# Two of the three one-column operations of attention's output norm go from GpSimd to VectorE

## The reference, cut to what matters

```
x = x + layernorm(attention(layernorm(x)))
x = x + layernorm(ffn(layernorm(x)))

def layernorm(x, eps=1e-05):
    m, v = mean(x), var(x)            # over the 128 columns
    return (x - m) / sqrt(v + eps)
```

```
local   = softmax(masked(q @ k.T * scale)) @ v
remote  = softmax(masked(rq @ rk.T)) @ rv @ rout_w + rout_b
gate    = sigmoid(local @ gl_w + remote @ gr_w)
result  = (gate * local + (1 - gate) * remote) @ out_w + out_b
```

## Time and profile before

| | |
|---|---|
| time, median of 3 runs | 557.9 us (557.33 to 559.46) |
| the profiled execution | 559.23 us |
| its span, first to last instruction | 557.4 us |
| mean granted TensorE clock | 0.956 |
| steady part of attention (s = 3 to 29) | about 110 to 341 us of the span |

### The profile page before, as it was taken

How to read it: one execution, slowest core, us unless ns; L and a number is a source line. 1 busy time by engine, 2 the same in 40 slices (tenths; PEclk the granted TensorE clock), 3 DMA queues, 4 the chain that set the end, 5 groups by cost and what they waited for, 6 DMA issues and landing times. The chain is left out here.

```text
span 557.4 us, 16662 instructions
## 1 busy us (share of the span) xinstructions
PE 506.9 (91%) x5277; PEld 312.7 (56%) x5280; DVE 424.0 (76%) x1954; ACT 298.3 (54%) x820; POOL 338.8 (61%) x799
## 2 busy tenths in 40 slices
PE   8878679999999999999999998869999999999991
PEld 3434324556556665555555665535677677577671
DVE  5986696988888888998899887645647777675655
ACT  2665305888888888888888888713212211211110
POOL 4799202688888888688888889960122343333241
PEclk9999855999999999999999999989999999999997
DMA  4466450332112332123331100000000000000001
GB/s 128 137 214 176 150 98 2 101 92 69 49 27 59 81 63 64 38 41 63 62 64 40 27 4 4 4 1 1 0 1 1 20 19 0 19 20 0 20 19 38
DMA packets 49058, 28.09 MB, mean 50 GB/s; under 512 B 6808, under 2 KB 48056, under 8 KB 48976
## 3 DMA queue, kind: packets, MB, share of 16 engines
q1 hardware_dynamic: 47648, 26.73, 19.0%
q10 hardware_dynamic: 1328, 0.36, 0.3%
HBM read 17.90 MB, written 8.91 MB: 48 GB/s over the span
## 5 line engine op out<-in xcount | busy, mean ns | idle before, releaser
L1096 DVE CUSTOM_DVE_ANT_0 added<-psS,maskq 128x256 bf16<-128x256 f32 x512 | 200.5, 414 | 34.8 <-PE psS L937 21.9
L1316 ACT ACTIVATE probs<-psST 128x512 f32<-128x512 f32 x240 | 143.2, 597 | 43.2 <-PE psST L973 41.7
L973 PE MATMUL psST<-qst,kst 50*128 50x128 bf16 x992 | 101.0, 222 | 0.0
L937 PE MATMUL psS<-kst,qst 48*128 48x256 bf16 x448 | 91.5, 286 | 2.4 <-DVE rowmax L1096 1.3
L994 PE MATMUL psPV<-probs,vst 128*10 128x128 f32 x1984 | 79.9, 277 | 11.9 <-POOL probs L1231 8.1
L1760 ACT ACTIVATE hT<-fpsH 128x512 f32<-128x512 f32 x32 | 19.1, 597 | 121.7 <-PE fpsH L1504 121.7
L1228 POOL TENSOR_SCALAR_AFFINE_SELECT probs<-probs 128x256 f32<-128x256 f32 x150 | 61.7, 412 | 4.3 <-ACT probs L1316 4.1
L1231 POOL TENSOR_SCALAR_AFFINE_SELECT probs<-probs 128x256 f32<-128x256 f32 x150 | 61.2, 408 | 0.0
L937 PEld LDWEIGHTS psS<-kst,qst 48*128 48x128 bf16 x448 | 25.2, 95 | 62.6 <-issue 36.3
L994 PEld LDWEIGHTS psPV<-probs,vst 128*10 128x10 f32 x1984 | 43.9, 91 | 27.1 <-issue 16.6
L973 PEld LDWEIGHTS psST<-qst,kst 50*128 50x128 bf16 x992 | 55.8, 95 | 0.0
(11 more groups left out here) (198 smaller groups left out, 1092.5 us busy)
## 6 DMA issues: line engine op xcount, KB each, us to landing
q_parts<-early SPq DMA_DIRECT2D x8, 384.0 KB, 2.6
k_parts<-early SPq DMA_DIRECT2D x8, 384.0 KB, 2.7
qst<-q_parts SPq DMA_DIRECT2D x32, 96.0 KB
kst<-k_parts SPq DMA_DIRECT2D x32, 96.0 KB
X<-in_L_attn_x_dram SPq DMA_DIRECT2D x8, 256.0 KB, 3.3
qst<-q_parts SPq DMA_DIRECT2D x32, 64.0 KB
kst<-k_parts SPq DMA_DIRECT2D x32, 64.0 KB
out_dram<-res SPq DMA_DIRECT2D x8, 256.0 KB, 2.3
```

Of the source, the lines that this page charges most:

```text
L937: last = nc.tensor.matmul(bank[:, a], q, kst[rows, slot, ring(n - 1, 2)], start=True, stop=True)
L973: last = nc.tensor.matmul(bank[:, a, side * P:(side + 1) * P], kst[rows, slot, ring(n - 1 + side)], qst[rows, slot, ring(n)], start=not ma ...
L1096: taken = nc.vector.tensor_tensor_reduce(added[:, 2 * (g % 2) + a], psS[g % 2][:, a], mask, 1.0, NEG * 4, ALU.add, ALU.max, rowmax[:, n.mo ...
L1316: nc.scalar.activation(probs[:, g ^ 1], psST[g % 2][:].rearrange("p a c -> p (a c)"), ACT.Exp, scale=SCALE).then_inc(s_exp.sem, 1)
```

## The change

The epsilon (`yve`) and the shift (`ybias`) move from POOL to DVE; the power (`yrstd`) stays on POOL. All three tiles get two buffers, and waits on block n - 1 become waits on block n - 2. `s_ystats` counts a third event (the epsilon), `s_yrstd` only the power, and the new `s_ybias` the shift.

```diff
-        yve = sb("yve", [P, 1])
-        yrstd = sb("yrstd", [P, 1])
-        ybias = sb("ybias", [P, 1])
+        yve = sb("yve", [P, 2, 1])
+        yrstd = sb("yrstd", [P, 2, 1])
+        ybias = sb("ybias", [P, 2, 1])
...
-        s_ystats = signal("s_ystats", "dve", 2)
-        s_yrstd = signal("s_yrstd", "pool", 3)
+        s_ystats = signal("s_ystats", "dve", 3)
+        s_yrstd = signal("s_yrstd", "pool")
+        s_ybias = signal("s_ybias", "dve")
...
+                    if (g, a) == (0, 1) and (s - 3).live:
+                        n = s - 3
+                        dve.wait_ge(s_ystats.sem, s_ystats.after(n, 2))
+                        dve.wait_ge(s_yrstd.sem, s_yrstd.after(n - 2))
+                        nc.vector.tensor_scalar(yve[:, n.mod(2)], ymv[:, n.mod(2), 1:2], EPS, None, ALU.add)\
+                          .then_inc(s_ystats.sem, 1)
+                    if (g, a) == (2, 0) and (s - 3).live:
+                        n = s - 3
+                        u = n.mod(2)
+                        dve.wait_ge(s_yrstd.sem, s_yrstd.after(n))
+                        dve.wait_ge(s_yn.sem, s_yn.after(n - 2))
+                        nc.vector.scalar_tensor_tensor(out=ybias[:, u], in0=ymv[:, u, 0:1], scalar=-1.0, in1=yrstd[:, u],
+                                                       op0=ALU.mult, op1=ALU.mult).then_inc(s_ybias.sem, 1)
...
                     pool.wait_ge(s_ystats.sem, s_ystats.after(n))
-                    pool.wait_ge(s_yn.sem, s_yn.after(n - 1))
-                    nc.gpsimd.tensor_tensor(yve[:], ymv[:, n.mod(2), 1:2], eps_col[:, 0:1],
-                                            ALU.add).then_inc(s_yrstd.sem, 1)
-                    pool.wait_ge(s_yrstd.sem, s_yrstd.after(n, 1))
-                    nc.gpsimd.tensor_tensor(yrstd[:], yve[:], mhalf[:, 0:1], ALU.pow).then_inc(s_yrstd.sem, 1)
-                    pool.wait_ge(s_yrstd.sem, s_yrstd.after(n, 2))
-                    nc.gpsimd.tensor_scalar(ybias[:], ymv[:, n.mod(2), 0:1], yrstd[:, 0:1], -1.0, ALU.mult,
-                                            ALU.mult).then_inc(s_yrstd.sem, 1)
+                    pool.wait_ge(s_yn.sem, s_yn.after(n - 2))
+                    nc.gpsimd.tensor_tensor(yrstd[:, n.mod(2)], yve[:, n.mod(2)], mhalf[:, 0:1], ALU.pow)\
+                      .then_inc(s_yrstd.sem, 1)
...
-                        act.wait_ge(s_yrstd.sem, s_yrstd.after(n))
+                        act.wait_ge(s_ybias.sem, s_ybias.after(n))
```

More of the change, by code:

```diff
@@ L1364, in emit @@
                         n = s - 3
-                        act.wait_ge(s_yrstd.sem, s_yrstd.after(n))
+                        act.wait_ge(s_ybias.sem, s_ybias.after(n))
                         act.wait_ge(s_x1.sem, s_x1.after(n - 1))
-                        nc.scalar.activation(yn[:], y[:, n.mod(2)], ACT.Identity, bias=ybias[:, 0:1],
-                                             scale=yrstd[:, 0:1]).then_inc(s_yn.sem, 1)
+                        nc.scalar.activation(yn[:], y[:, n.mod(2)], ACT.Identity, bias=ybias[:, n.mod(2)],
+                                             scale=yrstd[:, n.mod(2)]).then_inc(s_yn.sem, 1)
             schedule(act, emit)
```

## The result

The changed kernel takes 552.96 us (median of 6 runs, 550.41 to 554.7), the kernel before 558.06 in the same session (6 runs, 557.33 to 559.46): a ratio of 0.990, interval 0.9875 to 0.9931. That is 5.1 us faster. The forecast was 547: the sign was right, 552.96 lies at the slow edge of the range (543 to 553), and of the 11 us worked out 5.1 came. The profiled execution took 553.63 us, span 551.8.

The account below looks back on a forecast made before the run. The prediction took GpSimd's queue between `lprob` and the third select to bound narrow steps. Narrow 4.7, wide 4.9, last steps 1.5, less 0.1 at the tail, made 11.0 us: 548.2 profiled, 547 for the median, range 543 to 553.

Parts of the forecast that it names:

- What bounds the kernel: Attention's narrow steps: GpSimd's queue from `lprob` to the third select, norm included, is on the 8.38 us loop.
- The handover in narrow steps: The power, waiting for VectorE's epsilon (0.15 plus 0.09 signal), starts when it does now; 0.36 of GpSimd's 0.63 us is won.
- The narrow loop of 8.02: Attention's 13 narrow steps: the loop from VectorE's epsilon takes 8.02 us instead of 8.38, 4.7 us in all.
- then 2.91 of VectorE's own order up to the next epsilon: Last term of a narrow step's loop: from the maximum of unit 6 to the next epsilon, 2.91 us of VectorE's order.
- The wide steps: Attention's 14 wide steps: 0.48 of stalls go, 0.13 returns at `proj`; 0.35 each (bounds 0.2 and 0.6), 4.9 us.
- The two operations on VectorE: Epsilon and shift, about 0.1 us each in VectorE's order, are hidden by its 0.21 idle; no stall at the shift.
- rival 1: Shift or epsilon collides with GpSimd, or the handover takes longer than 0.24 us: 550.5 to 555 us, chance 0.17.
- Steps 30 and 31 and the tail: Attention's last two full steps gain 1.0 and 0.5 us; the last shift, behind VectorE's `xf` operations, costs 0.1.
- The feed-forward part only starts sooner.: The block behind attention's end starts earlier; a difference of 0 was forecast for its length.
- 2 (free handover): Rival: the handover costs nothing and GpSimd's whole 0.63 us a step counts, 17.7 us: 540 us, chance 0.07.
- 3 (nothing): Rival: GpSimd's time goes into waits for `both` and `lrs`, another loop being as long: within 0.5%, 557 us, chance 0.07.
- 4 (slower): Rival: VectorE stalls at the shift with the maxima of units 2 to 7 behind it: 562 us, chance 0.04.

Follow-up runs that it names:

- e8: Changed kernel with the shift back on GpSimd, so only the epsilon is on VectorE: 552.35 us, ratio 0.9896 to the kernel before.
- e9: Changed kernel with the epsilon back on GpSimd, so only the shift is on VectorE: 551.04 us, ratio 0.9876 to the kernel before.
- e3: Changed kernel with ScalarE's copy of `pvs` one unit earlier: 552.68 us, one execution.
- e13: Changed kernel with the local part of `both` one maximum earlier on VectorE: 549.53 us, ratio 0.9824 to the kernel before.
- e11: Kernel before with ScalarE's copy of `pvs` one unit earlier and nothing else: 560.27 us, one execution.
- e1: Changed kernel with GpSimd's power replaced by a multiplication of the same shape (norm's scale then wrong): 551.78 us, ratio 0.9888 to the kernel before.
- e12: Changed kernel with `pvs` copied one unit earlier, `psMix` behind the transposes of `pvs`, and 25 instead of 11 filler products at attention's end: 548.24 us.
- e15: Changed kernel with `pvs` copy and both parts of `both` earlier, `psMix` behind the transposes of `pvs`, 25 fillers at attention's end: 544.55 us, ratio 0.9743 to the kernel before.
- e2: Changed kernel with VectorE's shift two units later: 553.49 us, ratio 0.9898 to the kernel before.
- e6: Changed kernel with 25 instead of 11 filler products for TensorE at attention's end: 550.24 us, ratio 0.9796 to the kernel before.
- e7: Kernel before with 25 instead of 11 filler products for TensorE at attention's end: 558.39 us, ratio 0.9988.

## Why the prediction was off, point by point

**What bounds the kernel.** Right. GpSimd's queue between `lprob` and the third select bounded a narrow step; shortening it made the step shorter, and all but one of TensorE's waits for the selects went.

**The handover in narrow steps.** Right in each number: `yve` took 0.15, the signal 0.08, the power started 0.23 behind `gate`'s old place in VectorE's order (243.92 to 244.15), the select 0.51 later. e8 and e9 show its sense: with both ahead of the select, the shift gave the steady gain, and the epsilon alone gave a narrow step nothing, since the power starts when it started anyway.

**The narrow loop of 8.02.** This step failed in its last term, "then 2.91 of VectorE's own order up to the next epsilon". The others held. In the step shown: epsilon to power 0.23 (forecast 0.24), power to select 0.51 (0.50), to the third select's end 3.10 (3.10), to the value product 0.15 (0.14), to the maximum of unit 6 at 249.05 1.14 (1.13). From there to the next epsilon (252.05) it is 3.00 and not 2.91. The sum is 8.13. The 2.91 was taken over from the old trace as VectorE's own, but it has TensorE's scores of unit 7 in it, and these stand behind `proj`. The forecast had `proj` wait for `both` in wide steps alone; in narrow ones it put that wait at nothing and gave no reason. It is 0.15, and between VectorE's second maximum of unit 6 and its first of unit 7 lie 0.64 us (249.49 to 250.13) where 0.53 were before (253.08 to 253.61).

Why is `both` late? Because the select's 0.36 reaches the product of G = 1 but not that of G = 0, and the forecast never asked what else the latter waits for. ScalarE in the kernel before, in the step of the earlier trace rows:

```profile
248.26 0.59 ACT L1338 ACTIVATE pvs<-psPV 128x512 f32<-128x512 f32 x1
```

That copy ended at 248.85; with the 0.15 between copy and product that the changed kernel shows, the product could have started at 249.00 in place of 249.14. The margin was 0.14, and the select came 0.36 earlier. So with the change another loop is the longest, 8.13 us: copy of `pvs`, value product, transposes of `pvs`, `both`, `proj` and back over TensorE's order. That it needs both of its waits is shown by e3 and e13: take out either one and the step is 8.03 or 8.02, and the last term of the forecast's loop is back at 2.91 in both traces. e11 shows that the first wait costs nothing as long as GpSimd is late; e1, that a shorter power doesn't shorten this loop. The way round the loop is argued from the rows. The term was 0.36 a step and measured 0.25, and the first two steps of the second batch gained nothing (8.26 and 8.34 before, 8.28 and 8.40 now; why is open). So 13 steps gave 2.7 instead of 4.7 us.

**The wide steps.** The two stalls of 0.48 did go, and the wait of `proj` for `both` came up as foreseen, with 0.17 instead of 0.13 (the signal takes 0.15 where 0.1 was put). The term "a wide step gains 0.35" failed on what it left out, a second wait: `psMix` stands 0.1 late for the copy of the row maxima. 0.48 - 0.17 - 0.1 = 0.21, and 0.22 was measured; 14 steps gave 3.2 instead of 4.9 us. That this lies above the lower bound of 0.2 is luck: the bound stood for other reasons. e13 shows the first of the two waits at its price (8.38 to 8.21 or a little more). The second alone was not taken away: e12 swapped it for the remote `both`, and e15, which removes both of these, shows 0.08.

**The two operations on VectorE.** Hidden, as forecast, with no idle time before `ybias` but in 2 of 32 steps (0.9 us in total). The epsilon costs VectorE 0.06 us in its order. The shift took 0.32 (median of 32), more than the 0.2 assumed. e2 shows that this costs nothing. It is rival 1's collision in kind, in a place with room for it; of rival 1 the time came true (550.5 to 555) but not the mechanism.

**Steps 30 and 31 and the tail.** Forecast 1.4, measured 2.0. The distances from step 30 to 32 fell by 1.3 us (1.5 forecast), those from step 32 to 34 by 1.4 (nothing forecast), of which 0.9 is the old execution's low clock there, and behind them the last shift, queued behind `xf`, cost 0.8 where the forecast had 0.1: it took `xf`'s place in time from the trace of before as given, but everything ahead of it came earlier and `xf`'s wait for GpSimd less so.

**"The feed-forward part only starts sooner."** The order of its work is unchanged, but its length is not fixed: it was 2.0 us longer in the changed kernel's profiled execution, and as long in e11 without the change. At what clock its first products run depends on where the low stretches lie; e6 and e7 show it: with TensorE kept at work the part takes 181.5 us in both kernels. By the 6.6 to 6.9 us that the change is worth without the clock, of the missing 5.9 us about 4.1 to 4.4 belong to the terms in attention. The other 1.5 to 1.8 are the clock's and the session's share in a difference of two medians; which of them is not shown.

**The rivals.** 2 (free handover) is out: in all 13 narrow steps the power starts 0.08 us behind the end of `yve`, and e1, which makes GpSimd's queue shorter still, gains nothing. 3 (nothing) and 4 (slower) didn't come, though 3 named the right kind of reason for most of the shortfall in the steps: another loop nearly as long, TensorE's and VectorE's, with GpSimd's time going into waits for `both`. The chances at the end of the forecast (0.88, 0.08, 0.05) add up to 1.01; for slower the list has 0.04.

## What to carry to other kernels

When a releaser comes earlier by some amount, look up for each instruction that it releases the second-latest releaser: the gain ends where that one stands, and the view of waits names only the last. Here the copy of `pvs` stood 0.14 us ahead of the select that the view named, and a third of a narrow step's gain hung on it. And when a stretch of the old trace is carried into a new sum as one engine's own work, look for the waits inside it: the 2.91 us held one for TensorE.

After a change that shifts a stage's end, compare the later stages with their own windows of granted clock, and in more than one execution, before anything is credited to the edit. And once a wait is gone, the cheapest next step may be a reordering: moving two VectorE operations by one place each, a ScalarE copy by one unit and `psMix` behind its neighbour took another 4.5 us off the way from step 3 to step 30 (e6 to e15), where the change had taken 5.9.

## What the runs showed of the hardware

The same one-column `scalar_tensor_tensor` took from 0.13 us, with GpSimd idle, to 0.35 beside a GpSimd select. This row of the changed kernel is the whole of it, the length in ns as min/median/max:

```profile
L1164 DVE SCALAR_TENSOR_TENSOR ybias<-ymv,yrstd x32: 128/321/348, 112.4 to 365.6; 128x1 f32<-128x1 f32 x32
```

What decides is how far into the select it starts. In the changed kernel 28 of the 32 shifts start beside a select, 0.07 to 0.26 us into it, and every one of them ends 0.41 or 0.42 us behind the select's start: 0.32 long when it starts 0.10 in (245.12 above, the select at 245.02), 0.22 at 0.20, 0.16 at 0.26. In e2, where the shift stands two units later, eleven start 0.26 us or more into a select and take 0.15 to 0.17. GpSimd, then VectorE, in e2:

```profile
239.00 0.41 POOL L1242 TENSOR_SCALAR_AFFINE_SELECT probs<-probs 128x256 f32<-128x256 f32 x1
```

```profile
239.26 0.16 DVE L1164 SCALAR_TENSOR_TENSOR ybias<-ymv,yrstd 128x1 f32<-128x1 f32 x1
```

So a shift that comes early in a select loses what is left of the select's first 0.26 us (an estimate: 0.42 less its own 0.155), 0.2 at most here. The Trainium skill, "SBUF — State Buffer", section "Who interferes with whom", says that two SBUF inputs on VectorE contend with a GpSimd instruction that reads SBUF; the shift agrees with it. It says too that a single SBUF input does not, outside some modes. The epsilon, with one input, kept to 134 to 154 ns, but only one of its 32 (134 ns) stands beside a select, so these runs hardly test that.

The kernels' own spread goes with the clock. Over 43 executions of the kernel before, in the four sessions of the experiments, the time ran from 554.9 to 563.6 us while the mean granted clock ran from 0.968 to 0.950; a straight line through them gives 0.43 us for each 0.001 of clock. At a clock of 0.960 this line gives 558.5 us, and the one through the changed kernel's six executions (0.955 to 0.962) 551.7, 6.8 us apart: a second way, beside e6, e7 and e11, to see the change without the clock.
